# A gated cross-attention and feed-forward block: inputs ahead of the gates, the norms' small steps on VectorE, and one transpose from the DMA to TensorE

## What is computed

```python
def _layernorm(x, axis=-1, eps=1e-05): return (x - mean(x)) / sqrt(var(x) + eps)

def xattn(memory, query, seq_mask, b):            # 8 heads of 32
    K, V = split(memory, 2, axis=2)
    logits = einsum('bhqd,bhkd->bhqk', Q * 32 ** -0.5, K) + b[0]
    logits = logits + -1e+30 * (1.0 - mask)
    return einsum('bhqk,bhkd->bhqd', softmax(logits), V)

def ffn(x, w_gate, w_up, w_down):                 # weights are integers / 127
    return (silu(x @ wg.T) * (x @ wu.T)) @ wd.T

x = x + tanh(g_xattn) * xattn(ctx, _layernorm(x), mask, b)
x = x + tanh(g_ffn) * ffn(_layernorm(x), w_gate, w_up, w_down)
```

## Time and profile before

| | us |
|---|---|
| median of 3 runs | 141.6 |
| the runs | 140.57, 141.6, 143.15 |
| span of the profiled execution, first to last instruction | 139.7 |
| TensorE busy | 129.5 |
| VectorE busy | 103.4 |
| GpSimd busy | 100.3 |
| ScalarE busy | 90.7 |

### The profile page before, as it was taken

One profiled execution on the slowest core, in us unless ns is written; L12 is line 12 of the kernel. 1 busy time (PEld: TensorE's weight loads), 2 busy tenths in 40 slices (PEclk: granted clock), 3 DMA queues, 4 the chain that ended last, 5 costly groups with the idle time before them and its releaser, 6 DMA issues.

```text
span 139.7 us, 3761 instructions
## 1 busy us (share of the span) xinstructions
PE 129.5 (93%) x1276; PEld 98.0 (70%) x1276; DVE 103.4 (74%) x273; ACT 90.7 (65%) x204; POOL 100.3 (72%) x179
## 2 busy tenths in 40 slices
...
GB/s 139 164 223 359 388 304 9 88 199 195 144 121 155 127 75 0 5 75 5 38 207 195 21 0 150 5 0 0 0 42 38 5 153 77 2 77 2 75 82 89
DMA packets 32033, 14.08 MB, mean 101 GB/s; under 512 B 25588, under 2 KB 31240, under 8 KB 32008
## 3 DMA queue, kind: packets, MB, share of 16 engines
...
...
## 4 chain that ended last, share of the span: by engine, by line
PE 71%; POOL 9%; DMA 7%; DVE 6%; issue 2%; SPq 2%; ACT 0%; POOLq 0%; ACTq 0%; DVEq 0%
PE ps L1426 31%; PE ps L1452 15%; PE ps L1352 4%; DMA x_sb<-in_x_dram 4%; PE ps L1358 4%; PE ps L1328 3%; PE ps L1330 3%; PE ps L1372 3%; PE ps L1283 3%; DMA n_t<-norm 2%; DVE max_cols L1076 2%; POOL rstd L635 2%; POOL q_parts L664 2%; DVE stats L936 2%; PE ps L1212 2%
## 5 line engine op out<-in xcount | busy, mean ns | idle before, releaser
L1426 PE MATMUL ps<-n_t,w_gu_t 128*128 128x256 f16 x384 | 47.7, 273 | 0.5 <-DMA n_t<-norm 0.5
L1426 PEld LDWEIGHTS ps<-n_t,w_gu_t 128*128 128x128 f16 x384 | 36.6, 98 | 6.7 <-DVE h L1131 1.6
L681 POOL TENSOR_TENSOR h<-h 128x256 f16<-128x256 f32 x48 | 31.5, 674 | 11.2 <-ACT h L843 11.2
L1120 DVE SCALAR_TENSOR_TENSOR gated<-tanh_h,ps 128x256 f32<-128x256 f32 x48 | 20.0, 416 | 13.7 <-ACT tanh_h L834 13.5
L834 ACT ACTIVATE tanh_h<-ps 128x256 f32<-128x256 f32 x48 | 18.4, 384 | 15.2 <-PE ps L1426 15.1
L1452 PE MATMUL ps<-w_d_t,h 128*128 128x256 f16 x192 | 24.9, 273 | 0.0
L786 ACT ACTIVATE probs<-ps,exp_bias 128x512 f32<-128x512 f32 x32 | 21.6, 689 | 4.5 <-PE ps L1330 4.1
L1076 DVE TENSOR_REDUCE max_cols<-ps 128x4 f16<-128x512 f32 x32 | 20.7, 683 | 3.8 <-PE ps L1283 3.0
L1131 DVE SCALAR_TENSOR_TENSOR h<-ps,gated 128x256 f32<-128x256 f32 x48 | 20.4, 424 | 2.0 <-DVE gated L1120 0.4
L843 ACT ACTIVATE h<-h 128x256 f16<-128x256 f32 x48 | 18.6, 412 | 2.6 <-DVE h L1131 2.3
L1452 PEld LDWEIGHTS ps<-w_d_t,h 128*128 128x128 f16 x192 | 18.3, 98 | 2.8 <-issue 0.8
...
## 6 DMA issues: line engine op xcount, KB each, us to landing
...
q_stacks<-q_parts SPq DMA_TRANSPOSE x12, 3.4
n_t<-norm SPq DMA_TRANSPOSE x7, 3.1
```

The source lines that it names most:

```text
L681: pool.tensor_tensor(h16[:, r % 2, m, 1, :], h32[:, n % NHB, :], h16[:, r % 2, m, 0, :], ALU.subtract).then_inc(h_low, 1)
L1120: mine(dve.scalar_tensor_tensor(out=gated[:, n % 2, :], in0=tanh_h[:, n % 2, :], scalar=1.0, in1=got[:, 0:SH], op0=ALU.add, op1=ALU.mult))
L1426: ins = pe.matmul(dst, lhs, rhs, start=(w == 0 and (k, l) == terms[0]), stop=(k, l) == terms[-1], skip_group_check=True)
```

## The change

1. On SP the loads of x2 and x3 stand ahead of the three gates, and x4, kv2, x5 ahead of the down weights.
2. GpSimd's var_eps and neg_mean go to VectorE, behind its bn_aggr. The halves 2 and 3, 4 and 5, 6 and 7 of the first norm are done as pairs: VectorE's statistics of both, one neg_mean, one var_eps of four columns, one power on GpSimd. Every norm has its own place for these small results, so the statistics no longer wait for older norms.
3. Half 0 leaves `N_BY_DMA`: TensorE turns its second norm (nt0), and ScalarE copies it out.
4. Two of the three steps of `eb` go from VectorE to ScalarE; a check step goes from the mask steps to `ck`; two memsets go to the wide program.
5. The lists of all engines are written in another order.

```diff
-N_BY_DMA = (0, 1, 2, 3, 4, 5, 6)
+N_BY_DMA = (1, 2, 3, 4, 5, 6)
...
+STATS_PAIRS = {(1, 2): (2, 3), (1, 4): (4, 5), (1, 6): (6, 7)}
+
+def halves_of(step):
+    kind, which, r = step
+    return (r,) if kind.startswith(WIDE) else STATS_PAIRS.get((which, r), (r,))
...
     "dve": """
-        sa0 fr kp0 sa1 na0 mc kr0 sa2 na1 du0 br mt ft du1 ks0 kp1 sa3 rm0.0 rm0.1 rm0.2 rm0.3 rm1.0 eb sa4 sa5 kp2
+        sa0 kp0 na0 sa1 mc kr0 mt br na1 du0 fr kp1 du1 ks0 ft rm0.0 eb rm0.1 rm0.2 rm0.3 sa2 rm1.0 sa4 rm1.1 rm1.2
...
             load_x(sp, 0)
             load_kv(sp, 0)
             load_x(sp, 1)
+            load_x(sp, 2)
             load_kv(sp, 1)
+            load_x(sp, 3)
             for n, g in enumerate((g_xattn, g_ffn, attn_b)):
                 sp.dma_start(gates[:, n:n + 1], g.partition_broadcast(P)).then_inc(gates_loaded, 16)
-            load_x(sp, 2)
...
                     if kind == "stats":
-                        place = plan.nth[step]
-                        pool.wait_ge(var_ready, place + 1)
-                        pool.tensor_scalar(var_eps[:, place % NLB, :], mv[:, place % NLB, :, 1], LN_EPS,
-                                           1.0 / Q_SCALE_SQ if step[1] == 1 else 1.0, ALU.add, ALU.mult
-                                           ).then_inc(var_eps_ready, 1)
...
+                        halves = halves_of(step)
+                        at = slice(small(step[1], halves[0]), small(step[1], halves[-1]) + 1)
+                        pool.wait_ge(var_ready, plan.nth[step] + 1)
+                        pool.tensor_tensor(rstd[:, at, :], var_eps[:, at, :],
+                                           neg_half[:, 0:2 * len(halves)].rearrange("p (h t) -> p h t", t=2),
+                                           ALU.pow).then_inc(rstd_ready, 1)
...
+                    elif kind == "exp_bias":
+                        act.wait_ge(gates_loaded, 48)
+                        act.wait_ge(shut_out_ready, 1)
+                        act.activation(exp_bias[:, :], exp_bias[:, :], ACT.Identity, scale=MASK_STEP, bias=gates[:, 2:3]
+                                       ).then_inc(shut_out_added, 1)
+                        act.wait_ge(shut_out_added, 1)
+                        act.activation(exp_bias[:, :], exp_bias[:, :], ACT.Relu, scale=-1.0, bias=gates[:, 2:3]
+                                       ).then_inc(shut_out_added, 1)
...
             def exp_bias_steps():
-                dve.wait_ge(gates_loaded, 48)
-                mine(dve.tensor_scalar(exp_bias[:, :], exp_bias[:, :], MASK_STEP, gates[:, 2:3], ALU.mult, ALU.add))
-                wait_mine()
-                dve.tensor_scalar(exp_bias[:, :], exp_bias[:, :], gates[:, 2:3], 0.0, ALU.subtract, ALU.min
-                                  ).then_inc(exp_bias_ready, 1)
+                dve.wait_ge(shut_out_added, 2)
+                dve.tensor_scalar(exp_bias[:, :], exp_bias[:, :], -1.0, None, ALU.mult).then_inc(exp_bias_ready, 1)
...
-                        for i in range(2):
-                            ins = dve.bn_aggr(mv[:, slot, i, :], stats[:, i, :])
-                        ins.then_inc(var_ready, 1)
+                        for h in halves:
+                            for i in range(2):
+                                mine(dve.bn_aggr(mv[:, small(which, h), i, :], stats[:, small(which, h), i, :]))
+                        wait_mine()
+                        at = slice(small(which, halves[0]), small(which, halves[-1]) + 1)
+                        if which == 2 or norm1_on_pool((step[0].replace("stats", "norm1"), r)):
+                            mine(dve.tensor_scalar(neg_mean[:, at, :], mv[:, at, :, 0], -1.0, None, ALU.mult))
+                        dve.tensor_scalar(var_eps[:, at, :], mv[:, at, :, 1], LN_EPS,
+                                          1.0 / Q_SCALE_SQ if which == 1 else 1.0, ALU.add, ALU.mult
+                                          ).then_inc(var_ready, 1)
```

164 lines of the change are left out of this document (82 added, 82 removed).

## The result

The changed kernel takes 143.05 us in the median (142.6 to 143.43, 4 runs) beside 141.81 of the kernel before (140.57 to 143.15, 4 runs). The forecast was 139.4 and its range ended at 141.6: it had the sign wrong.

A forecast was written before the change was run, and what follows sets the result against it. Bound: TensorE's nearly closed stream from hi0.0, after a VectorE-GpSimd relay. Swap 1.1, GpSimd -0.3, start 1.1, less 0.22 for ks2.0 and 0.3 gaps: net 1.4, span 138.3, plus 1.1 around it, 139.4 us; range 136.9 to 141.6.

The forecast's parts named there:

- the stream: TensorE's matmuls from hi0.0 on: ks2.0 adds 0.22 us and gaps 0.3, with bounds 0 and 1.5 for gaps.
- The start: VectorE and GpSimd up to at0.1: the new order brings at0.1's end 1.1 us ahead.
- so rm0.0 starts at 14.65: VectorE's first row maximum: na1 at 10.1 plus 4.55 us, 2.6 ahead of before.
- at0.1 ends at 31.5: GpSimd's addition: at0.0 on VectorE at 29.05, then power, la3 and two additions; 1.1 us ahead of 32.64.
- Rival 4: TensorE's clock falls over rm0 and rm1 as well, costing 2 us: 141.4; chance 0.06.
- GpSimd from at0.1 to lb0: The new order takes 6.39 us there against 6.07 before, a loss of 0.3.
- The swap: Half 0's second norm turned by TensorE, not DMA: hi0.0 2.32 us behind lb0 instead of 3.43, gaining 1.1.
- What cost nothing: Removed memsets, later gates (near 11.7), exp_bias steps on ScalarE, paired statistics and weight turns: all hidden, no cost.
- the lock: VectorE's small steps can be caught by GpSimd's two-input steps, taking about 1 us; la0's catch and 0.5 counted.
- rival 1: Every small VectorE step meeting GpSimd is caught, in start and stream, eating the 1.4 us gain: 141.0; chance 0.12.
- rival 3: VectorE bounds the stream through second norms' new steps and catches, up to 9.5 us: 149, or 145; chance 0.07.
- rival 2: No catch and a four-column power at 0.71 us in the start: hi0.0 at 38.6, time 137.8; chance 0.30.

The follow-up runs named there:

- e1: Changed kernel with 28 first warm-up matmuls ahead of mt in place of 14: median 141.69 us, ratio 1.0022 to the kernel before.
- e5: Changed kernel with 28 first warm-up matmuls, la3 ahead of sa6's power and du3 ahead of at0.0: median 140.26 us, ratio 0.9962 to before.
- e3: Changed kernel with la3 ahead of sa6's power on GpSimd and du3 ahead of at0.0 on VectorE: median 142.02 us, ratio 1.0006 to before.
- e6: Changed kernel with ha5 and hb0 ahead of mx2 on ScalarE: median 142.78 us, ratio 1.0109 to before.
- e7: Kernel before with the swap alone (nt0 on TensorE, no DMA for half 0) and ks2.0 behind hi0.0: median 140.89 us, ratio 0.9914.

## Why the prediction was wrong, step by step

The forecast of 139.4 missed the profiled run's 143.22 by 3.82: hi0.0 2.39 late, the stream 0.61, the time around the span 0.8.

1. **The start failed**, at "so rm0.0 starts at 14.65" and "at0.1 ends at 31.5". The step took TensorE's rate from before and counted VectorE's instructions alone. Behind the hole ahead of mt, of which wu1's place is 0.65 us, the clock fell over qs0.0, ft, wu2 and rm0.0: 2.15 us at rm0.0, of which e1, with the hole filled, gave back 1.94. The same sum is near at the whole clock, 14.86 in e1 and 14.93 in e5, but in part by luck: in e1 na1 is at 9.71, 0.4 ahead of the 10.1 forecast, and from there to rm0.0 it is 5.15 and not 4.55. The 0.6 is a catch that the sum did not have: fill_row, moved behind du0, met la1 and took 1.27 for 0.55, and TensorE waited 1.35 us for it. Rival 4 named the mechanism with a chance of 0.06, and cost it at rm0 and rm1; it struck earlier. From rm0.0 to at0.0 I had 14.4 and it is 12.9: a pair of statistics with its small steps is over after 2.1 us, not 2.35, and no catch came there. So at0.0 was 0.63 late, and at0.1, with la3 behind a power of 1.17 and additions of 1.60 on GpSimd, 1.47.
2. **The q of half 3 was left out.** The sum counts la3 as 1.16 us ahead of at0.0. It does not ask who waits for du3, which went behind at0.1 and ended at 32.39 instead of 29.0, nor for its DMA and rm3.0. e3 prices that at 1.15 of hi0.0. It is the wait that took the place of the one removed.
3. **GpSimd from at0.1 to lb0**: 6.39 forecast, 7.16 found; without the wait for hb0 it is 6.30 in e5. The sum was right, and e6 shows that the wait cost nothing: TensorE's queue ended later.
4. **The swap**: 2.32 behind lb0 forecast, 2.46 found; worth 0.7, not 1.1, since in the new order the DMA's way is 3.2. In the old order (e7) TensorE's own queue left nothing of it. The Trainium skill's prices for one square in "VectorE: DVE Perf Modes", section "The three transpose paths", 390 and 1309 ns, would have made the swap of eight squares worth 7.4 us, an estimate that no run here bears out.
5. **The stream**: 0.52 forecast, 1.13 found: 0.22 of ks2.0, three gaps of 0.22 to 0.28 behind VectorE, and 0.16 in small pieces. Two of the gaps are at pairs of hidden steps that wait for its product, as the pair of 2.16 us at 117.68 (1.92 in the earlier trace rows); the third is do4.0, which waits for its sum fi3. Mis-sized, within its bounds.
6. **The time around the span**: I took 1.1, between the 0.9 and the 1.9 that the runs allowed. It is 1.8 to 1.9 in every run here, so the profiled execution of before was the one at 141.6. With 1.9 the forecast's span of 138.3 would have given 140.2; e5, with the two missed steps undone, has that span of 138.3, and 140.26 in the median; that the spans agree is luck, as its hi0.0 is 0.55 ahead of the forecast and its stream 0.6 longer.
7. **What cost nothing** did: the last gate was there by 11.2, exp_bias took 0.16 on VectorE. Of the lock, sa1's var_eps was caught as forecast (0.94); the other small steps up to lb0 took 0.16 to 0.19: those at 4.7, 21.3 and 23.9 with GpSimd waiting for them, those at 28.0 and 34.1 beside a norm of GpSimd, which has one tensor as input. In the stream two more of the 24 were caught, beside a two-input step: 0.34 at 67.73 and 0.65 at 95.21. So rival 1 came with three steps of 24, and of rival 3 there are the three gaps, 0.75 us in all. Two ends of the range are not the sums they name: rival 2 with a closed stream is 137.8 - 0.3 = 137.5, and rival 4 is 141.4.
